# A second buffer for the turned probabilities in a wide cross-attention, and an earlier place for ScalarE's copy of the folded values

## The reference

```python
N_HEAD, MODEL_DIM, KEY_DIM, VALUE_DIM = (16, 128, 64, 64)
q = (query @ Wq + bq).reshape(b, sq, N_HEAD, KEY_DIM)
k = (key @ Wk + bk).reshape(b, key.shape[1], N_HEAD, KEY_DIM)
v = (value @ Wv + bv).reshape(b, value.shape[1], N_HEAD, VALUE_DIM)
scores = jnp.einsum('bqhd,bkhd->bhqk', q, k) / TEMP
attn = jax.nn.softmax(scores, axis=-1)
out = jnp.einsum('bhqk,bkhd->bqhd', attn, v).reshape(b, sq, N_HEAD * VALUE_DIM)
out = out @ Wo + bo + residual
mu = jnp.mean(out, axis=-1, keepdims=True)
var = jnp.var(out, axis=-1, keepdims=True)
return (out - mu) * jax.lax.rsqrt(var + EPS) * ln_gamma + ln_beta
```

## Time and profile before

| | |
|---|---|
| median of 3 runs | 1540.04 us (1539.15 to 1540.40) |
| profiled execution, its own time | 1538.09 us |
| its span (first to last instruction) | 1536.4 us |
| TensorE busy / mean granted clock | 1326.9 us (86%) / 0.933 |
| VectorE, ScalarE, GpSimd busy | 1054.9, 918.9, 878.6 us |
| the 16 tiles of the last attention | about 1086 to 1193 us of the span |

### The profile page before, as it was taken

How to read it: one execution, slowest core, us unless ns; L and a number is a source line. 1 busy time by engine, 2 the same in 40 slices (tenths; PEclk the granted TensorE clock), 3 DMA queues, 4 the chain that set the end, 5 groups by cost and what they waited for, 6 DMA issues and landing times. The chain is left out here.

```text
span 1536.4 us, 23960 instructions
## 1 busy us (share of the span) xinstructions
PE 1326.9 (86%) x7572; PEld 1006.5 (66%) x7572; DVE 1054.9 (69%) x2133; ACT 918.9 (60%) x1391; POOL 878.6 (57%) x619
## 2 busy tenths in 40 slices
PE   8789999797788888779579999998787349999998
PEld 7767777465365666646468887884456338787786
DVE  6534444596699999889756666775564766666665
ACT  4468887553787887477346665555554327555554
POOL 3168888400899999632047775661345028665665
PEclk9689999897899999899689999999999669999999
DMA  6021111000000000040054346443000134444443
GB/s 251 1 60 46 42 48 27 2 2 1 1 1 1 1 0 0 3 165 1 1 126 128 127 126 174 127 128 122 1 1 1 55 80 130 121 130 123 130 120 85
DMA packets 51557, 103.25 MB, mean 67 GB/s; under 512 B 6248, under 2 KB 10928, under 8 KB 49936
## 3 DMA queue, kind: packets, MB, share of 16 engines
q1 hardware_dynamic: 51472, 102.17, 22.3%
HBM read 99.99 MB, written 2.16 MB: 66 GB/s over the span
## 5 line engine op out<-in xcount | busy, mean ns | idle before, releaser
L1541 POOL TENSOR_TENSOR RA<-RW 128x1024 f32<-128x1024 f32 x128 | 246.7, 1965 | 87.6 <-ACT RW L1502 87.6
L881 ACT ACTIVATE PS<-PS 128x512 f32<-128x512 f32 (+1 forms) x260 | 151.1, 582 | 216.2 <-PE PS L677 215.6
L974 POOL TENSOR_TENSOR l3f_hid_rest<-RW,l3f_hid_high 128x512 fp32r<-128x512 f32 x132 | 170.4, 1291 | 142.7 <-ACT l3f_hid_high L873 142.7
L974 POOL TENSOR_TENSOR l2f_hid_rest<-RW,l2f_hid_high 128x512 fp32r<-128x512 f32 x128 | 165.3, 1292 | 137.2 <-ACT l2f_hid_high L873 137.2
L974 POOL TENSOR_TENSOR l0f_hid_rest<-RW,l0f_hid_high 128x512 fp32r<-128x512 f32 x128 | 165.3, 1292 | 64.6 <-ACT l0f_hid_high L873 57.9
L934 DVE TENSOR_TENSOR RW<-RW,PS 128x512 f32<-128x512 f32 (+1 forms) x260 | 178.7, 687 | 11.6 <-DVE RW L929 0.9
L1572 PE MATMUL PS<-identf,RA 128*128 128x128 f32 x1024 | 139.3, 286 | 37.5 <-DVE RA L1463 33.4
L1572 PEld LDWEIGHTS PS<-identf,RA 128*128 128x128 f32 x1024 | 116.6, 145 | 74.2 <-DVE RA L1463 71.1
L1463 DVE SCALAR_TENSOR_TENSOR RA<-RA,RW,PS 128x1024 f32<-128x1024 f32 x128 | 157.0, 1277 | 11.0 <-ACT PS L1508 10.4
L1508 ACT ACTIVATE PS<-RA 128x1024 f32<-128x1024 f32 x128 | 130.1, 1026 | 54.2 <-DVE RA L1463 51.6
L934 DVE TENSOR_TENSOR RW<-RD,PS 128x512 f32<-128x512 f32 x128 | 87.9, 687 | 107.2 <-ACT PS L881 98.6
(11 more groups left out here) (344 smaller groups left out, 3286.7 us busy)
## 6 DMA issues: line engine op xcount, KB each, us to landing
RD<-l2f_kept SPq DMA_DIRECT2D x128, 256.0 KB, 3.6
RB<-l3f_kept SPq DMA_DIRECT2D x128, 256.0 KB, 3.7
RD<-l0f_kept SPq DMA_DIRECT2D x32, 256.0 KB, 3.1
RA<-in_w SPq DMA_DIRECT2D x2, 2048.0 KB, 11.6
RA<-in_wg SPq DMA_DIRECT2D x2, 1024.0 KB, 9.4
RA<-in_wu SPq DMA_DIRECT2D x2, 1024.0 KB, 11.4
RA<-in_wd SPq DMA_DIRECT2D x2, 1024.0 KB, 13.4
RC<-in_wg SPq DMA_DIRECT2D x1, 2048.0 KB, 7.9
```

The costliest lines, as they stand in the source:

```text
L881: act.activation(gate, gate, e.func, bias=st.bias).then_inc(e.acted, 1)
L974: pool.tensor_tensor(rest, hid, high, ALU.subtract).then_inc(e.hidden_ready, 1)
L1541: pool.tensor_tensor(*pair_scores(r, h), ALU.add).then_inc(added, 1)
```

## The change

`PT` becomes two buffers used by turns, the old one in RW and one in RA at 2048 to 3071 (the place of the value weights `wv`, which are read for the last time ahead of the loop). The copy then waits for the output two tiles back in place of that one tile back. On ScalarE the store of the folded values runs one number further ahead: three come before the loop in place of two, and in the loop tile t stores number t+3, behind its copy and finish and in front of the exponential of tile t+2; the finish of tile t moves from the end of the tile's work to right behind the copy. TensorE's order, VectorE's and SP's stay as they are.

```diff
-    PT = RW[:, 2 * HC:3 * HC]
+    PT = [RW[:, 2 * HC:3 * HC], RA[:, 2048:3072]]
...
-            for n in range(2):
+            for n in range(3):
                 store_vw(n)
             act.wait_ge(ahead.loaded, ahead.count)
             for t in range(2):
                 ahead.round(act, ahead.span(0, t))
             for t in range(NT):
-                if t + 2 < 2 * B:
-                    store_vw(t + 2)
                 act.wait_ge(p_turned, t + 1)
-                if t >= 1:
-                    act.wait_ge(out_ready, t)
-                act.activation(PT, turn_ps, ACT.Copy).then_inc(p_stored, 1)
+                if t >= 2:
+                    act.wait_ge(out_ready, t - 1)
+                act.activation(PT[t % 2], turn_ps, ACT.Copy).then_inc(p_stored, 1)
+                ahead.finish(act, t, ahead.span(t // 4, t % 4))
+                if t + 3 < 2 * B:
+                    store_vw(t + 3)
                 if t + 2 < NT:
                     exp(t + 2)
                     ahead.round(act, ahead.span((t + 2) // 4, (t + 2) % 4))
-                ahead.finish(act, t, ahead.span(t // 4, t % 4))
...
-                    mm = pe.matmul(out_ps[t % 2], PT[:, bass.ts(j, P)], VW[:, t // 2, j, :],
+                    mm = pe.matmul(out_ps[t % 2], PT[t % 2][:, bass.ts(j, P)], VW[:, t // 2, j, :],
```

## The result

The changed kernel took 1522.42 us (median of 4 runs, 1521.45 to 1523.66) against 1540.22 us for the kernel before timed beside it (4 runs, 1539.15 to 1543.20): 0.9894 of the time, 95% interval 0.9870 to 0.9919. The forecast was 1524.5 us, 1520 to 1530. In two later comparisons with more runs the same kernel came to 0.9913 (0.9881 to 0.9945) and 0.9918 (0.9892 to 0.9945).

The account below looks back on a forecast made before the run. Bound by a ring in the last attention: ScalarE's copy waited for the output one tile back, 6.51 us a tile. Gains of 11.4 to turn 14 and 4.2 after, 15.6 us off the median 1540.04, gave 1524.5, range 1520 to 1530.

Parts of the forecast that it names:

- What bounds: Last attention, 16 tiles: ScalarE's copy waits for the previous tile's output, the next fold for the copy; 6.51 us a tile.
- Second buffer: Attention loop: copy starts 1.07 us behind the turn, hidden by the output with 0.4 us to spare; TensorE's own round 5.1.
- K: TensorE's time in the attention loop from a turn to the next scores: 3.30 us, 3.26 to 3.36, at most 3.42.
- What is late next: Attention loop: every second turn waits for GpSimd's multiply; turns alternate 6.18 and 5.12 us, a tile 5.65 in the mean.
- The road: From scores of tile t+1 over VectorE's maximum and GpSimd's multiply to the turn of tile t: 8.0 us.
- The reordering: ScalarE's store and exponential in the attention loop: covered by 2.7 us, the rounding by 0.7; costs nothing.
- Turn 14: Start of tile 14's turn in the last attention: 1168.44 against 1179.81, 11.4 us gained, 11.65 to 10.5 over the bounds.
- The last two tiles: From tile 14's turn to the last output's end: 7.6 us against 11.75, gain 4.2, or 2.7 if the clock falls.
- The row at 604.43: Elsewhere in the kernel, behind 2.87 us of waiting, 16 transposes took 2.28: upper clock level, leaning to 1524.5 over 1526.0.
- Sum: Whole last attention: 11.4 + 4.2 = 15.6 us gained; 1522.5 for the profiled run, 1524.5 off the median.
- Growing road: Rival in the attention loop: GpSimd's multiply held by VectorE's work beside it, a tile 6.25 us, 1532.4 us; chance 0.05.
- The slower one: Rival: TensorE's clock falls inside the attention loop, 9.6 us a tile, 1580 us; chance 0.02.

Follow-up runs that it names:

- the buffer-only run: Changed kernel with the second buffer but ScalarE's old order: 1524.76 us, 0.9899 of the kernel before.
- The two runs that shorten and lengthen the road: Changed kernel with VectorE's sum of the tile before ahead of the next maximum: 1521.47 us, 0.9877; with VectorE's maximum done twice: 1535.65 us, 0.9996.
- the one that closes a ring over one tile: Changed kernel with VectorE's add of a finished output and its statistics moved in front of the sum: 1541.21 us, 1.0033 of the kernel before.
- both halves: Second buffer with ScalarE's old order: 1524.76 us, 0.9899 of the kernel before; ScalarE's new order with one buffer: 1538.02 us, 0.9992.
- the first profile: Profiled run of the changed kernel from its first comparison: 1521.66 us, stage 126.70 us against 140.33 before.
- the second profile: The unaltered changed kernel run again: median 1524.28 us, 0.9913 of the kernel before; stage 127.12 us.

## Why the prediction was right

- *What bounds.* Right. The copy's wait for the output closed the ring, and one buffer more opened it; the buffer-only run shows that nothing else was needed.
- *Second buffer.* Right: copy at turn + 1.10 (forecast 1.07), fold straight behind the output. TensorE's round was put at 5.12 and is 5.17 to 5.20, since K, from turn to the next scores, is 3.38 in the profile after (1103.89 to 1107.27) and not 3.30; it lies between the bounds given, 3.26 and 3.42.
- *What is late next.* Right, and the term that mattered most: without it the forecast would have been 1518. The road measures 2.02 + 3.98 + 1.90 + 0.10 = 8.00 (1107.27 to 1109.29, to 1113.27, to 1115.17, to 1115.27). Two tiles take 11.38 (1103.89 to 1115.27), forecast 11.30. The two runs that shorten and lengthen the road, and the one that closes a ring over one tile, show it as cause.
- *The reordering.* Right at nothing, by both halves.
- *Turn 14.* 10.84 us gained (84.29 less 73.45), forecast 11.4, within its bounds of 10.5 and 11.65; the difference is seven times the 0.08 in K.
- *The last two tiles.* Right in size at either clock: 11.75 less 8.93 is 2.8 (forecast 2.7 with a fallen clock), and less 7.60 it is 4.15 (forecast 4.2). The size with a fallen clock came out of other pieces than forecast: turn 15 stands 4.32 behind turn 14, forecast 4.42, but as 1.29 + 3.03 and not 1.73 + 2.69, because the clock was still at 1.00 for the first 0.47 us. The choice between the two failed in the profiled run: behind a wait of 2.33 us the clock fell to 0.50. In three other profiles with the same loop (two of the changed kernel, one with the buffer only) it stayed at the upper level. The row at 604.43 was a fair lean and no rule.
- *Sum.* 15.6 forecast for the stage, 13.6, 13.2 and 13.2 measured in the three profiles. That the three are so alike is chance: the first lost 1.3 us behind turn 14, the other two 1.75 on the way to turn 1, where the forecast had no change; with neither, the parts give 10.84 + 4.15 = 15.0. The medians differ by 17.8, 15.3 and 9.6 us in the three comparisons; that the first came so near is partly luck, since 3.0 us of its profile lay ahead of the stage. Why the third is only 9.6 where its stage gained 13.2 stays open.
- *The rivals.* Growing road: the multiply still takes 1.90, also where it runs beside the next maximum (1113.27 and 1114.46), no sign of it. The slower one: the loop held a clock of 1.00 (1085 to 1160 of the first profile); what does make it slower than before is not the clock but a ring over one tile.

## What to carry to other kernels

A second buffer is worth the distance to the next ring, not the wait that it removes: here 1.26 us of idle TensorE per tile became 0.82 us of gain (6.51 to 5.69). Write down for each engine's step what it waits for and how many tiles a chain spans until it comes back to itself: a chain over two tiles costs half of its length per tile, one over one tile all of it, and 0.45 us of work at a wrong place in an in-order engine's stream can close the shorter one. Where a small change sits in a long kernel, judge it by its own loop, which repeats to 0.01 us here, and not by the total.

## What the runs showed of the hardware

The granted clock of TensorE isn't settled by the program alone. Behind the same 2.33 us of waiting it fell to 0.50 in one execution of the changed kernel and stayed at 1.00 in another, and the 1.75 us by which "to turn 1" differs are of the same kind: the scores of tile 2 run for the most part at 1.2 GHz in the second profile and at 2.4 GHz in the first, with the same instructions ahead of them. The first profile, then the second:

```profile
1084.51 1.13 PE L1920 MATMUL PS<-RA,XT 128*128 128x512 f32 x2
```
```profile
1083.37 1.88 PE L1920 MATMUL PS<-RA,XT 128*128 128x512 f32 x2
```

The stretches of the second profile around this:

```profile
1082.00:1083.30 1.30, 0.58 (x20) 0.43 (x16) 0.00 (x0) 0.60 (x1) 0.00 (x0) 1.00 0.00 0
1083.90:1086.80 2.90, 2.90 (x5) 0.94 (x4) 0.00 (x0) 1.13 (x3) 1.13 (x1) 0.50 0.00 0
```

Ahead of these scores TensorE did three short folds of 0.67 us each, from 1079.95 on, with waits of 0.72 to 0.78 us ahead of them. The clock was still at 1.00 during the folds and fell once the scores were running; in the first profile's turn 14, too, it fell only after TensorE was back at work. Ahead of turn 14 of the kernel before it was down from the start. Why it falls in one execution and not in another isn't shown.
